# Choosing two experts from the capped weights on all partitions, and letting TensorE address the expert weights

## The reference

```
logits = jnp.mean(x, axis=1) @ Wr + br
routing_weights = jax.nn.softmax(logits, axis=-1)
capacity = float(math.ceil(N * CAPACITY_FACTOR / E))
expected_loads = routing_weights.sum(axis=0) * (N / B)
scale = jnp.where(expected_loads > capacity, capacity / expected_loads, 1.0)
routing_weights = jax.nn.softmax(routing_weights * scale, axis=-1)
top_w, top_i = jax.lax.top_k(rw_tok, K)
top_w = jax.nn.softmax(top_w, axis=-1)
h = jax.nn.gelu(jnp.einsum('nd,edf->enf', xf, W1) + b1[:, None, :], approximate=False)
y = jnp.einsum('enf,efd->end', h, W2) + b2[:, None, :]
out = jnp.einsum('ne,end->nd', w_dense, y).reshape(B, S, D)
out = _layer_norm(out + x, gamma, beta)
```

## Time and profile before

| what | value |
|---|---|
| median of 3 runs | 113.6 us (113.43 to 113.66) |
| span of the profiled execution | 110.6 us |
| median less span | 3.0 us |
| mean granted TensorE clock | 0.895 |
| PE busy | 85.7 us (77%) |
| DVE busy | 77.3 us (70%) |
| ACT busy | 69.6 us (63%) |
| POOL busy | 60.8 us (55%) |
| loop over the rows ends, routing begins | about 84 us |
| experts' first matmul (L1080) | 92.19 us |
| experts' second stage begins (L1092) | 94.43 us |
| last matmul ends | about 103.4 us |

### The profile page before, as it was taken

How to read it: one execution, slowest core, us unless ns; L and a number is a source line. 1 busy time by engine, 2 the same in 40 slices (tenths; PEclk the granted TensorE clock), 3 DMA queues, 4 the chain that set the end, 5 groups by cost and what they waited for, 6 DMA issues and landing times.

```text
span 110.6 us, 3220 instructions
## 1 busy us (share of the span) xinstructions
PE 85.7 (77%) x1034; PEld 62.0 (56%) x1034; DVE 77.3 (70%) x272; ACT 69.6 (63%) x195; POOL 60.8 (55%) x114
## 2 busy tenths in 40 slices
PE   3941036875949899999999999998999599999300
PEld 2730003553727577777777776776588375789300
DVE  0550197999998988898888888898237533277971
ACT  5010345257988999888898889956724486447330
POOL 2380049870433473554764757645355682998970
PEclk9999755558999999999999999999999859999855
DMA  2123695000000000000000000000000000000123
GB/s 50 37 71 90 158 231 124 3 0 0 6 0 0 3 6 0 6 0 3 6 0 0 12 0 6 0 0 6 0 0 0 0 6 0 0 3 0 46 63 81
DMA packets 8232, 2.81 MB, mean 25 GB/s; under 512 B 6426, under 2 KB 8090, under 8 KB 8218
## 3 DMA queue, kind: packets, MB, share of 16 engines
q1 hardware_dynamic: 6826, 2.27, 9.1%
q10 hardware_dynamic: 1392, 0.36, 1.3%
HBM read 2.10 MB, written 0.52 MB: 24 GB/s over the span
## 4 chain that ended last, share of the span: by engine, by line
PE 55%; DVE 15%; DMA 8%; POOL 7%; issue 5%; ACT 3%; SPq 3%; POOLq 1%; DVEq 0%; ACTq 0%
PE bank L948 8%; DMA w_in<-in_L_conv_Wkv 8%; PE bank L906 7%; PE bank L896 6%; PE bank L958 4%; PE bank L1005 4%; DVE stack L501 4%; PE bank L920 4%; PE bank L1092 3%; PE bank L885 3%; PE bank L967 3%; PE bank L886 3%; POOL rstd L707 3%; PE bank L930 3%; PE bank L1080 3%
## 5 line engine op out<-in xcount | busy, mean ns | idle before, releaser
L501 DVE TENSOR_REDUCE stack<-bank 128x4 f16<-128x512 f32 x32 | 20.9, 691 | 1.9 <-PE bank L906 1.9
L329 ACT ACTIVATE prob<-bank 128x512 f32<-128x512 f32 x32 | 18.9, 595 | 2.8 <-PE bank L930 1.2
L779 POOL TENSOR_TENSOR og<-og,rden 128x128 f32<-128x128 f32 x16 | 6.4, 402 | 21.2 <-DVE og L520 21.2
L769 POOL TENSOR_TENSOR stack<-qkg,stack 128x256 f16<-128x256 f32 x16 | 10.8, 673 | 6.9 <-ACT qkg L307 6.7
L493 DVE COPY qk_t<-bank 128x1024 f16<-128x1024 f16 x16 | 11.0, 688 | 4.4 <-PE bank L896 4.4
L707 POOL TENSOR_TENSOR rstd<-rstd,neg_half 128x4 f32<-128x4 f32 x12 | 12.6, 1053 | 1.0
L1005 PE MATMUL bank<-ones,ident 128*128 128x256 f16 x68 | 11.2, 330 | 1.9 <-POOL ident L788 1.9
L906 PE MATMUL bank<-qk_t 48*128 48x128 f16 x128 | 11.9, 229 | 0.9 <-DVE qk_t L493 0.9
L885 PE MATMUL bank<-w_hi,x_t 128*128 128x512 f16 x16 | 7.0, 435 | 6.8 <-DVE w_lo L563 5.4
L896 PEld LDWEIGHTS bank<-ident,stack 128*128 128x128 f16 x128 | 9.5, 106 | 4.5 <-issue 1.3
L896 PE MATMUL bank<-ident,stack 128*128 128x128 f16 x128 | 10.8, 232 | 0.0
(11 more groups left out here) (113 smaller groups left out, 200.9 us busy)
## 6 DMA issues: line engine op xcount, KB each, us to landing
w_in<-in_L_ffn_W SPq DMA_DIRECT2D x3, 256.0 KB, 3.8
x_all<-in_x SPq DMA_DIRECT2D x4, 128.0 KB, 4.0
out<-res SPq DMA_DIRECT2D x3, 128.0 KB, 2.0
b_b<-in_L_ffn_b SPq DMA_DIRECT2D x1, 256.0 KB, 3.6
w_in<-in_L_conv_Wkv SPq DMA_DIRECT2D x2, 64.0 KB
out<-res ACTq DMA_DIRECT2D x1, 128.0 KB, 2.0
w_in<-in_L_conv_Wq SPq DMA_DIRECT2D x1, 64.0 KB
bg_b<-in_L_conv_bg ACTq DMA_DIRECT2D x1, 64.0 KB, 6.3
```

The source lines that it names most:

```text
L329: nc.scalar.activation(prob[:, s % 2, a], s2_p[a], ACT.Exp, scale=HD ** -0.5).then_inc(exp_done[a], 1)
L501: nc.vector.tensor_reduce(q[:, :, a, SHIFT], s1_p[a], AX, ALU.max, negate=True).then_inc(max_done[a], 1)
L769: nc.gpsimd.tensor_tensor(stack_slots(b, 2, 1), qkg[:, b, 0:2 * INNER].rearrange("t (a h c) -> t a h c", a=2, h=HEADS), stack_slots(b, 0, ...
```

## The change

All routing numbers are now computed on all 128 partitions alike. The mean becomes `mean_rep` (64 x 128, each column the mean), so that the matmul with `Wr` gives the logits on every partition. The first softmax isn't divided out: `r_capped = min(exp, cap * sum)` has the order of the capped weights, and the two largest are taken from it. The second softmax is then an exponential with scale `1/sum` of the sorted values; the third, over two numbers, is a tanh of half their gap. So `shares` needs no matmul to spread it. TensorE reads the experts' numbers into its own registers and takes its first weights straight from `w1_split`; the copy to `w1_sel` goes. ScalarE has no `copy_tn_t(2)` and `(3)` any more, VectorE has them. On TensorE `transpose_tn(3)` stands behind fc1(0), and the idle matmuls of the routing are 2 rounds instead of 5. On GpSimd `add_beta(0)` and `(1)` stand in the loop's steps 19 and 20, `(2)` and `(3)` behind `tn_b2`.

```diff
-WARM_START, WARM_NORM, WARM_ROUTING = 7, 1, 5
+WARM_START, WARM_NORM, WARM_ROUTING = 7, 1, 2
...
-        logits_p = bank[B_PROJ][0:1, 0:EXPERTS]
-        shares_p = bank[7][:, 0:2]
+        logits_p = bank[B_PROJ][:, 0:EXPERTS]
...
-            high_t(3)
-            exponentials(0, logits_p, EXPERTS)
-            copy_tn_t(2)
-            exponentials(1, capped[0:1, :], EXPERTS)
-            copy_tn_t(3)
-            exponentials(2, top_v[0:1, 0:2], 2)
-
+            act.wait_ge(r_max, 1)
+            nc.scalar.activation(r_exps[:, :], logits_p, ACT.Exp, bias=r_neg_max[:, 0:1],
+                                 accum_out=r_sum[:, 0:1]).then_inc(r_exp, 1)
+            high_t(3)
+            act.wait_ge(top_v_ok, 1)
+            nc.scalar.activation(r_second[:, :], top_v[:, :], ACT.Exp, scale=r_inv[:, 0:1],
+                                 accum_out=r_sum[:, 1:2]).then_inc(r_second_ok, 1)
             nc.scalar.activation(table_warm[:, :], neg_half[:, 0:1], ACT.Gelu)
+            act.wait_ge(r_gap_ok, 1)
+            nc.scalar.activation(r_tanh[:, :], r_gap[:, :], ACT.Tanh, scale=0.5).then_inc(r_tanh_ok, 1)
...
             dve.wait_ge(mean_done, 1)
-            nc.vector.tensor_scalar(mean_col[:, :], mean_p, 1.0 / TOKENS, None, ALU.mult).then_inc(mean_ok, 1)
+            nc.vector.tensor_scalar(mean_rep[:, :], ones[0:DIM, :], mean_p, 1.0 / TOKENS, ALU.mult, ALU.mult).then_inc(mean_ok, 1)
             dve.wait_ge(logits_done, 1)
-            nc.vector.tensor_reduce(soft_max[0:1, 0:1], logits_p, AX, ALU.max, negate=True).then_inc(r_max, 1)
+            nc.vector.tensor_reduce(r_neg_max[:, 0:1], logits_p, AX, ALU.max, negate=True).then_inc(r_max, 1)
+            dve.wait_ge(tc_ok, CHUNKS)
+            dve.wait_ge(rstd2_ok, CHUNKS)
+            nc.vector.tensor_tensor(tn[:, r, :], tc[:, r, :], rstd2[:, r].unsqueeze(2).broadcast_to(WIDE),
+                                    ALU.mult).then_inc(tn_ok, 1)
...
+            then_next(nc.vector.scalar_tensor_tensor(out=r_capped[:, :], in0=r_sum[:, 0:1].broadcast_to([TOK, EXPERTS]),
+                                                     scalar=CAPACITY / TOKENS, in1=r_exps[:, :],
+                                                     op0=ALU.mult, op1=ALU.min))
+            nc.vector.max(top_v[:, :], r_capped[:, :])
+            then_next(nc.vector.reciprocal(r_inv[:, 0:1], r_sum[:, 0:1]))
+            dve.sem_inc(top_v_ok, 1)
+            nc.vector.max_index(top_i[:, :], top_v[:, :], r_capped[:, :]).then_inc(top_i_ok, 1)
+            dve.wait_ge(r_second_ok, 1)
+            then_next(nc.vector.reciprocal(r_inv[:, 1:2], r_sum[:, 1:2]))
+            nc.vector.scalar_tensor_tensor(out=r_gap[:, :], in0=r_second[:, 0:1], scalar=r_second[:, 1:2],
+                                           in1=r_inv[:, 1:2], op0=ALU.subtract, op1=ALU.mult).then_inc(r_gap_ok, 1)
...
+            copy_tn_t(2)
+            copy_tn_t(3)
+            dve.wait_ge(r_tanh_ok, 1)
+            nc.vector.tensor_scalar(shares_b[:, 0:1], r_tanh[:, :], 0.5, 0.5, ALU.mult, ALU.add)
+            then_next(nc.vector.tensor_scalar(shares_b[:, 1:2], r_tanh[:, :], -0.5, 0.5, ALU.mult, ALU.add))
+            dve.sem_inc(shares_b_ok, 1)
             dve.wait_ge(top_i_ok, 1)
             expert = [dve.value_load(top_i[0:1, j:j + 1], min_val=0, max_val=EXPERTS - 1) for j in range(2)]
-
-            dve.wait_ge(w1_split_ok, EXPERTS // 2)
-            for j in range(2):
-                nc.vector.tensor_copy(w1_sel[:, j], w1_split[:, :, bass.ds(expert[j], 1), :].rearrange(
-                    "c l e f -> c l (e f)")).then_inc(w1_sel_ok, 1)
...
+                if t in (19, 20):
+                    add_beta(t - 19)
             power_t(2)
...
             transpose_tn(2)
-            transpose_tn(3)
 
             stay_warm(bank[B_U][:, 0:256], ones[:, :].bitcast(F16), WARM_ROUTING)
+
+            pe.wait_ge(w1_split_ok, EXPERTS // 2)
+            pe.wait_ge(top_i_ok, 1)
+            expert = [pe.value_load(top_i[0:1, j:j + 1], min_val=0, max_val=EXPERTS - 1) for j in range(2)]
...
             fc1(0)
-
-            pe.wait_ge(shares_ok, 1)
-            nc.tensor.matmul(shares_p, ones[0:1, :], shares[0:1, :], start=True, stop=True).then_inc(shares_done, 1)
+            transpose_tn(3)
             fc1(1)
```

More of the change, by code:

```diff
@@ L125, in metaformer_kernel @@
         t_beta = sb("t_beta", [TOK, ROWS, DIM])
[L127 to L137, removed]
+        mean_rep = sb("mean_rep", [DIM, TOK])
+        r_exps = sb("r_exps", [TOK, EXPERTS])
+        r_capped = sb("r_capped", [TOK, EXPERTS])
+        r_second = sb("r_second", [TOK, EXPERTS])
+        r_neg_max = sb("r_neg_max", [TOK, 1])
+        r_sum = sb("r_sum", [TOK, 2])
+        r_inv = sb("r_inv", [TOK, 2])
+        r_gap = sb("r_gap", [TOK, 1])
+        r_tanh = sb("r_tanh", [TOK, 1])
+        top_v = sb("top_v", [TOK, EXPERTS])
+        top_i = sb("top_i", [TOK, EXPERTS], U32)
+        shares_b = sb("shares_b", [TOK, 2])
         b2_pick = sb("b2_pick", [TOK, 2, DIM])
@@ L140, in metaformer_kernel @@
         b2_sel = sb("b2_sel", [TOK, DIM])
-        w1_sel = sb("w1_sel", [2 * DIM, 2, 2, HID], F16)
         w2_sel = sb("w2_sel", [HID, 2, DIM])
@@ new lines, in copy_tn_t @@
+            def copy_tn_t(c):
+                dve.wait_ge(tn_tp, c + 1)
+                nc.vector.tensor_copy(tn_t[:, c * CHUNK:(c + 1) * CHUNK, :], tn_tp_p[c]).then_inc(tn_t_ok, 1)
+            dve.wait_ge(tn_t_ok, 2)
+            copy_tn_t(2)
[3 more added lines that the diff above has]
+            then_next(nc.vector.tensor_scalar(shares_b[:, 1:2], r_tanh[:, :], -0.5, 0.5, ALU.mult, ALU.add))
@@ L619, in _ @@
+            dve.sem_inc(shares_b_ok, 1)
             dve.wait_ge(top_i_ok, 1)
             expert = [dve.value_load(top_i[0:1, j:j + 1], min_val=0, max_val=EXPERTS - 1) for j in range(2)]
-            dve.wait_ge(w1_split_ok, EXPERTS // 2)
-            for j in range(2):
-                nc.vector.tensor_copy(w1_sel[:, j], w1_split[:, :, bass.ds(expert[j], 1), :].rearrange(
-                    "c l e f -> c l (e f)")).then_inc(w1_sel_ok, 1)
-            dve.wait_ge(r_exp, 3)
-            then_next(nc.vector.reciprocal(soft_inv[0:1, 2:3], soft_sum[0:1, 2:3]))
@@ L824, in _ @@
             low_t(3)
-            for c in range(CHUNKS):
-                add_beta(c)
             pool.wait_ge(top_i_ok, 1)
@@ L846, in _ @@
                                         ALU.add).then_inc(tn_b2_ok, 1)
+            add_beta(2)
+            add_beta(3)
             for c in range(CHUNKS):
@@ L1053, in _ @@
             pe.wait_ge(ld["br"], 16)
-            nc.tensor.matmul(logits_p, ones[0:1, 0:1], br_row[0:1, :], start=True, stop=False)
+            nc.tensor.matmul(logits_p, ones[0:1, :], br_row[0:1, :], start=True, stop=False)
             for c in range(CHUNKS):
@@ L1061, in _ @@
             pe.wait_ge(mean_ok, 1)
-            nc.tensor.matmul(logits_p, mean_col[:, :], wr[:, :], start=False, stop=True).then_inc(logits_done, 1)
+            nc.tensor.matmul(logits_p, mean_rep[:, :], wr[:, :], start=False, stop=True).then_inc(logits_done, 1)
             transpose_tn(2)
-            transpose_tn(3)
             stay_warm(bank[B_U][:, 0:256], ones[:, :].bitcast(F16), WARM_ROUTING)
+            pe.wait_ge(w1_split_ok, EXPERTS // 2)
+            pe.wait_ge(top_i_ok, 1)
+            expert = [pe.value_load(top_i[0:1, j:j + 1], min_val=0, max_val=EXPERTS - 1) for j in range(2)]
+            w1_pick = [[w1_split[:, part, bass.ds(expert[j], 1), :].rearrange("c e f -> c (e f)") for part in range(2)]
+                       for j in range(2)]
             def fc1(c):
@@ L1072, in fc1 @@
                     n = 2 * c + j
-                    if c == 0:
-                        pe.wait_ge(w1_sel_ok, j + 1)
-                    if n in (2, 4):
-                        pe.wait_ge(tn_t_ok, n // 2 + 2)
-                    if n == 7:
-                        pe.wait_ge(shares_b_ok, 1)
+                    if n == 4:
+                        pe.wait_ge(tn_t_ok, CHUNKS)
+                    if n == 0:
+                        pe.wait_ge(r_exp, 1)
                     for part in range(2):
-                        last = nc.tensor.matmul(bank[n][:, :], w1_sel[:, j, part, :],
+                        last = nc.tensor.matmul(bank[n][:, :], w1_pick[j][part],
                                                 tn_t[:, c * CHUNK:(c + 1) * CHUNK, :].rearrange("c s t -> c (s t)"),
```

19 lines of the change are left out of this document (6 added, 13 removed).

## The result

| | before | after |
|---|---|---|
| median | 113.62 us (113.43 to 113.66) | 118.38 us (118.22 to 119.42), 4 runs |
| ratio | | 1.0451 [1.0405, 1.0497] |
| span of the profiled execution | 110.6 us | 115.4 us |
| mean granted clock | 0.895 | 0.825 |
| choice of experts ends | 90.13 | 89.64 |

What follows compares the result with a forecast made beforehand. It took routing, then TensorE's unbroken run from fc2(0), to bound what could move: fc2(0) 1.57 us late behind late register reads, plus 0.85 from a second clock dip, +2.4 on 113.6 gives 116.0 us, range 113.8 to 116.9.

Steps and rivals of the forecast that it cites:

- Late reads behind the shares: VectorE ahead of w2_sel: register reads queue behind the shares and take 1.65 us, so fc2(0) starts 1.57 late.
- `w2_sel` 0.42: VectorE's scaling of the second weights ahead of fc2(0): takes 0.42 us, as before, ending at 95.9.
- From the mean to the choice: Routing: removing a softmax round trip and a scaling brings the choice of experts about 1.0 us earlier, to 89.1.
- TensorE's reads: Between choice and fc1(0): TensorE's two register reads take 1.6 us, so fc1(0) starts at 90.75, 1.44 earlier.
- Rival D: Register reads cost only 0.69 us, where the engine has no work: 112.3 us, or 113.3 at low clock; chance 0.12.
- fc2 at the low clock: fc2(1) in a clock dip: its weight loads already set the pace, so +0 taken from +0 to +1.8 us.
- The second dip itself: After TensorE's pause and fc2(0): clock likely falls near 97.7, fc1(2) takes 1.71 us instead of 0.86, +0.85.
- `add_beta` ahead of the mean: GpSimd before the mean: two add_beta of 0.71 us each delay power_t(3), +0.15 us, between 0 and 0.2.
- covered: GpSimd behind tn_b2: add_beta(2) and (3) end near 99.5, when rstd3 wants to start; without cover at most 0.3 us.
- The sum: fc2(0) late by 1.57 us plus 0.85 from the second clock dip: end shift +2.4, span 113.0, time 116.0.
- The 3.0 us "around the span": Whole time: 3.0 us lie around the profiled span of 110.6 against the median of 113.6, added to the new span.

Runs made afterwards that it cites:

- a_early: Changed kernel with VectorE's two register reads moved ahead of its copies of tn_t: 114.7 us, ratio 1.0229 to the kernel before.
- b_late_2: Kernel before with a second pair of VectorE register reads behind the shares, used for w2_sel: 115.21 us, ratio 1.0203.
- a_w2first: Changed kernel with GpSimd's tn_b2 waiting until w2_sel is written: 116.52 us, ratio 1.0258 to the kernel before, resting on two executions.
- after_2: Changed kernel measured again, unaltered: 117.95 us, ratio 1.0373 to the kernel before.
- b_late_warm2: Kernel before with second VectorE register reads behind the shares and 2 rounds of idle matmuls instead of 5: ratio 1.0395 over its shorter executions (117.3 to 119.0 us).
- a_fill_2: Changed kernel with 3 rounds of idle matmuls added between fc1(1) and fc2(0): 115.66 us, ratio 1.0166 to the kernel before.
- a_warm5: Changed kernel with 5 rounds of idle matmuls in the routing instead of 2: 117.09 us, ratio 1.0394 to the kernel before.
- a_early_warm5: Changed kernel with VectorE's register reads ahead of its copies of tn_t and 5 rounds of idle matmuls: 114.88 us, ratio 1.0196 to the kernel before.

## Why the prediction was half right

**Late reads behind the shares.** Right in place and nearly in size: 1.87 us to issue against 1.65 forecast, and both a_early and b_late_2 show the cost. Named as the new wait, with what queues behind it.

**`w2_sel` 0.42.** Failed. The step took the duration from a place where `tn_b2` had not begun. In the new place `tn_b2`, which starts from the same shares, meets it: +0.76 (a_w2first). The prediction itself has `tn_b2` from about 95.3 and `w2_sel` from 95.5; I read GpSimd's row for its own end only. The Trainium skill's page "SBUF — State Buffer", section "SBUF: two separate sides", says that some of VectorE's operations and GpSimd's share a pair of ports that one instruction holds to its end, while the other waits. The rows agree for `tn_b2`: 248 to 255 ns apart from it (a_w2first), 496 and 760 beside it. Not every instruction of GpSimd does this: beside the small `b_part`, which ran from 93.90 in the kernel before, the two still took 0.42.

**From the mean to the choice.** The parts removed were worth what I said (1.15 against 1.0), but the clock was taken from the earlier trace rows, where it fell at 87.4. Here it fell near 85.3, and the sum over the tokens (1.02 instead of 0.60) and the logits (0.59 instead of 0.38) became slow. Of 1.03 us expected of the choice, 0.49 came. I treated one execution's moment of falling as a property of the kernel; it is not: in after_2 the same code kept the clock until 86.4, and the choice ended at 88.95, earlier than the forecast's 89.1.

**TensorE's reads.** Forecast 1.6 (1.65 from 89.1 to 90.75), measured 1.90 from the end of the choice to the first matmul: +0.25 to 0.3. The loads themselves were about right (0.49 and 0.32 against 0.54 and 0.31). Rival D, that only 0.69 of them would show, fell. The Trainium skill's floor of about 600 ns per load ("DMA: Bandwidth & Descriptors", "Latency and other measured facts") isn't borne out: 490 and 320 ns on TensorE.

**fc2 at the low clock.** Failed, and the costliest where the clock stays low. "fc2's matmuls already start at the pace of their loads" was argued, and I took +0 of a bound of +1.8. At 1.2 GHz the loads stretch as well. fc2's weight loads, first in b_late_2 (fc2 all at 2.4 GHz), then in b_late_warm2 (mostly at 1.2), ns min/median/max:

```profile
L1093 PEld LDWEIGHTS bank<-w_sel,hid x64: 186/192/192, 96.3 to 105.0; 128*128 128x128 f32 x64
L1093 PEld LDWEIGHTS bank<-w_sel,hid x64: 192/333/337, 98.0 to 112.1; 128*128 128x128 f32 x64
```

So 16 matmuls take 3.31 to 3.65 instead of 1.75 to 1.97. In the profiled execution the dip hit only parts of fc2(0) (2.40) and fc2(1) (2.13), which with fc1(2) (1.71, as forecast) makes 1.66 instead of 0.85; in after_2 it hits all of fc2(0).

**The second dip itself.** Right in the profiled execution, where the clock fell near 99.0 against the forecast's 97.7; in after_2 it had not come back before. Filling the hole buys back 2.3 us against the changed kernel of the same set (a_fill_2). The hole is not enough by itself, though: in a_warm5 the clock stood through 2.92 us of it.

**GpSimd.** `add_beta` ahead of the mean cost nothing (`rstd2` of the last chunk ended at 86.00, before 86.03): `power_t(3)` took 1.32 instead of 1.55. Behind `tn_b2`, "covered" was true of the changed kernel and false once fc2(0) came earlier (a_early, a_early_warm5, a_w2first).

**The sum.** 1.57 + 0.85 = 2.4 forecast; 3.19 + 1.66 = 4.85 came. The missing 1.62 at fc2(0) is 0.76 of `w2_sel`, 0.54 of the choice, which the low clock held up, 0.25 of TensorE's reads; VectorE's reads were 0.22 longer too, and the steps between fc1(0) and the shares 0.21 shorter, which cancels; the rest, under 0.1, is not resolved. The missing 0.81 is fc2. The range's upper end, 116.9, was said to be for a slow fc2(1), but the prediction's own bound of +1.8 for it gives 117.8; and it allowed nothing for an earlier fall of the clock or for the meeting with `tn_b2`.

The 3.0 us "around the span" were misread too. In the later sets the kernel before took 1.7 to 2.3 us more than its own span, and its executions at a mean clock of 0.895 to 0.897 took 111.8 to 112.6. So the profile that the prediction reads is of a shorter execution than the median of 113.6, one with a late fall of the clock. The forecast adds its shift to the median, so this did not enter the sum, only the choice of the moment at which the clock falls.

What stays open: what decides at which moment the clock falls in one execution and not in another. The runs show that it varies, not why.

## What to carry to other kernels

Read registers as soon as the number exists, in idle time of the engine that needs them; behind a wait, a pair costs 1.4 to 1.9 us here, and its engine's queue with it. Idle matmuls ahead of a chain of thin matmuls should be priced by what the low clock would cost over the whole stage behind them, not by the idle time that they fill. Where a step is moved, take its duration beside what the other engines do at its new place, and look again at everything called covered once the repair has brought the stage forward.
